# Last feed-forward stage of a transformer block: its buffers, routing and first two samples' work placed among the last slots of attention

## The reference

```python
x = x + 0.5 * ffn(layernorm(x), Wr, br, W1, b1, W2, b2)
x = x + attention(layernorm(x), Wqkv, Wo)          # 16 heads of 16, rotary, causal
x = x + 0.5 * ffn(layernorm(x), Wr, br, W1, b1, W2, b2)

def ffn(x, ...):                  # per sample b:
    scores0 = x[:, 0, :] @ Wr + br                 # routing by row 0 of a sample
    _, idx = top_k(scores0, 2)                     # 2 of 8 experts
    h = gelu(x @ W1[idx] + b1[idx])                # 256 -> 2 x 256
    return sum_k(h @ W2[idx] + b2[idx]) / 2
```

## Time and profile before

| | |
|---|---|
| median of 3 runs | 2322.23 us (2321.12 to 2323.56) |
| the profiled execution, its own time | 2318.06 us |
| its span, first to last instruction | 2316.4 us |
| PE busy | 2134.5 us, 92% |
| DVE, ACT, POOL busy | 1919.7, 1358.9, 1299.7 us |
| mean granted clock of TensorE | 0.987 |
| attention's last slots and the join | about 1845 to 1961 us of the span |

### The profile page before, as it was taken

How to read it: one execution, slowest core, us unless ns; L and a number is a source line. 1 busy time by engine, 2 the same in 40 slices (tenths; PEclk the granted TensorE clock), 3 DMA queues, 4 the chain that set the end, 5 groups by cost and what they waited for, 6 DMA issues and landing times. The chain is left out here.

```text
span 2316.4 us, 53401 instructions
## 1 busy us (share of the span) xinstructions
PE 2134.5 (92%) x18194; PEld 1160.0 (50%) x18194; DVE 1919.7 (83%) x3973; ACT 1358.9 (59%) x2568; POOL 1299.7 (56%) x1460
## 2 busy tenths in 40 slices
PE   5999998799999999999999999999999986999999
PEld 2666665344444444444444444444444434666666
DVE  6777776688999899899989998998999854777776
ACT  4545544166667666666666666666667653555553
POOL 6666666454555455455545545554555435666664
PEclk9999999899999999999999999999999988999999
DMA  6766665444445434444544454444445413666665
GB/s 206 205 199 204 199 194 183 109 88 88 96 98 100 95 93 97 88 92 93 102 90 95 96 99 92 92 97 88 93 98 100 89 56 119 194 203 200 203 204 165
DMA packets 280391, 295.32 MB, mean 127 GB/s; under 512 B 45784, under 2 KB 263224, under 8 KB 280120
## 3 DMA queue, kind: packets, MB, share of 16 engines
q1 hardware_dynamic: 280120, 291.90, 50.1%
HBM read 140.08 MB, written 83.89 MB: 97 GB/s over the span
## 5 line engine op out<-in xcount | busy, mean ns | idle before, releaser
L996 ACT ACTIVATE probs<-bank 128x512 f32<-128x512 f32 x1280 | 747.8, 603 | 460.5 <-PE bank L1104 454.1
L929 DVE TENSOR_REDUCE at_mx<-bank 128x1 f32<-128x512 f32 (+3 forms) x1408 | 838.8, 634 | 137.9 <-PE bank L1086 137.9
L850 POOL TENSOR_SCALAR_AFFINE_SELECT probs<-probs 128x512 f32<-128x512 f32 x512 | 320.4, 638 | 671.4 <-ACT probs L996 667.7
L1104 PE MATMUL bank<-stacks 49*128 49x512 f16 (+3 forms) x2048 | 460.9, 303 | 72.9 <-ACT probs L996 70.9
L1081 PE MATMUL bank<-stacks 48*128 48x512 f16 (+3 forms) x2048 | 491.2, 302 | 26.0 <-DVE at_mx L929 13.1
L587 ACT ACTIVATE probs<-bank,b1s 128x512 f32<-128x512 f32 x256 | 176.1, 688 | 371.2 <-PE bank L652 362.7
L1104 PEld LDWEIGHTS bank<-stacks 49*128 49x128 f16 x2048 | 136.1, 94 | 461.0 <-ACT probs L996 338.3
L1086 PE MATMUL bank<-mask,turn 64*128 64x128 bf16 (+2 forms) x1408 | 341.0, 242 | 0.0
L652 PE MATMUL bank<-stacks 128*128 128x512 f16 x768 | 175.5, 386 | 25.4 <-DVE stacks L529 25.3
L1081 PEld LDWEIGHTS bank<-stacks 48*128 48x128 f16 x2048 | 157.7, 94 | 72.3 <-DVE at_mx L929 47.0
L856 POOL TENSOR_TENSOR turned<-turned,at_sin 128x512 f32<-128x512 f32 x128 | 176.5, 1379 | 30.8 <-DVE turned L904 30.8
(11 more groups left out here) (127 smaller groups left out, 4071.5 us busy)
## 6 DMA issues: line engine op xcount, KB each, us to landing
stacks<-qk_image SPq DMA_DIRECT2D x384, 128.0 KB, 4.5
qk_image<-v_qk SPq DMA_DIRECT2D x128, 256.0 KB, 4.1
stacks<-w_hi SPq DMA_DIRECT2D x192, 128.0 KB, 3.7
stacks<-w_lo SPq DMA_DIRECT2D x192, 128.0 KB, 3.8
b2s<-in_b SPq DMA_DIRECT2D x128, 128.0 KB, 3.9
after_ffn<-probs SPq DMA_DIRECT2D x32, 512.0 KB, 6.5
at_x<-after_ffn SPq DMA_DIRECT2D x32, 512.0 KB, 4.0
late_x<-after_ffn SPq DMA_DIRECT2D x32, 512.0 KB, 4.7
```

The source lines that it names most:

```text
L850: nc.gpsimd.affine_select(out=ap, in_=ap, compare_op=ALU.is_ge, fill=0.0, base=0, pattern=[[0, d] for d in dims] + [[1, P]], channel_multi ...
L929: nc.vector.tensor_reduce(o_ap, i_ap, AX_X, ALU.max).then_inc(max_done, 1)
L996: nc.scalar.activation(probs[:, c, :], st_ps[c % 2][:], ACT.Exp, scale=DH ** -0.5).then_inc(exp_done, 1)
L1104: ins = nc.tensor.matmul(bank[:, col:col + T - q0], k_stack[ss.par][rows, j + ha, kt * P:(kt + 1) * P], q_stack[ss.par][rows, j + ha, q0:T ...
```

## The change

Buffers: `of_last_ffn` lays the last stage's W1, W2 and xT buffers on `stacks0`, `h` on the half of `v0_qk` that held q and k, `h32` and two of `res` on `turned`, the third of `res` on `probs`; sample 31 uses none of the stacks among these, so most waits name sample 30 now. The ones row gets a tile of its own. Routing on PE and DVE is cut into three pieces, and the first two samples' work moves to earlier slots:

| after slot | PE | DVE | ACT | POOL | SP |
|---|---|---|---|---|---|
| 120 | | | | | inputs, x(0), x(1) |
| 123 | | route_rows, norm_stats(0) | | route(0) | |
| 124 | route_turn | route_turned | | norm(0) | |
| 125 | route_logits | route_top, norm_stats(1) | | | |
| 126 | transposes(0) | xT_low(0) | xT_high(0) | norm(1) | routes, load_first(0) |
| 127 | | | | | load_second(0) |
| 128 | times_w1(0), j 0 to 2 | | | | load_first(1) |
| 129 | times_w1(0), j 3; transposes(1) | xT_low(1) | xT_high(1) | residual(0) | load_second(1) |
| 130 | times_w1(1) | norm_stats(2), h_low(0) | gelu(0) | norm(2) | load_x(2) |
| 132 | transposes(2), times_w2(0), route(1) | step(1) ... | step(1) ... | step(1) ... | load_x(3), finish, rows(1), step(1) ... |

The core of the diff (what is left out changes names only):

```diff
+    def of_last_ffn(self):
+        s0, s1 = self.stacks[0][:, 0:8, :], self.stacks[0][:, 8:16, :]
+        bits = self.v0_qk[:].bitcast(F16).rearrange("p (j n) -> p j n", n=T)
...
+        xT = [self.xT0, Split(s0[:, 4:6, :], s0[:, 6:8, :])]
+        w1 = [self.w1_0, Split(s0[:, 0:2, :], s0[:, 2:4, :])]
+        w2 = [Split(s1[:, 4 * i:4 * i + 2, :], s1[:, 4 * i + 2:4 * i + 4, :]) for i in range(2)]
+        h32 = [self.turned[:, j, :] for j in range(4)]
+        h = [Split(bits[:, 8 * i:8 * i + 4, :], bits[:, 8 * i + 4:8 * i + 8, :]) for i in range(2)]
...
             if before and s == 1:
-                sp.wait_ge(before.st_done, 40 * B)
+                sp.wait_ge(before.st_done, 40 * (B - 1))
...
             if before and s == 0:
-                act.wait_ge(before.pv_done, 16 * B)
+                act.wait_ge(before.pv_done, 16 * (B - 1))
+                act.wait_ge(before.qk_lo, 4 * B)
...
             if before and s == 1:
+                pe.wait_ge(before.res_done, 2 * (B - 1))
+            if before and s == 2:
                 pe.wait_ge(before.res_done, 2 * B)
...
-            for j in range(4):
+            for j in js:
+                if before and s == 0 and j == 0:
+                    pe.wait_ge(before.max_done, 44 * B)
+                    pe.wait_ge(before.mt_copied, 4 * B)
+                if before and s == 0 and j == 3:
+                    pe.wait_ge(before.exp_done, 40 * B)
...
-            if n.b == B - 1:
-                pe.wait_ge(own.next.xT_lo, NC)
+            if n.b >= B - 2:
+                pe.wait_ge(own.next.xT_lo, NC * (n.b - B + 3))
...
@@ vector
-            at.slot(At(0, B), 0)
-            f2.route(0)
+            for g in range(1, 4):
+                at.slot(At(0, B - 2), g)
+            f2.route_rows(0)
             f2.norm_stats(0)
+            at.slot(end, 0)
+            f2.route_turned(0)
+            at.slot(end, 1)
+            f2.route_top(0)
             f2.norm_stats(1)
-            at.slot(At(0, B), 1)
+            at.slot(end, 2)
             f2.xT_low(0)
...
+            at.slot(over, 1)
+            f2.xT_low(1)
+            at.slot(over, 2)
+            f2.norm_stats(2)
+            f2.h_low(0)
+            at.slot(over, 3)
+            at.slot(over + 1, 0)
+            for s in range(1, B):
                 f2.step(s)
@@ tensor
+            f2.route_turn(0)
+            at.slot(end, 1)
+            f2.route_logits(0)
+            at.slot(end, 2)
             f2.transposes(0)
+            at.slot(end, 3)
+            at.slot(over, 0)
+            f2.times_w1(0, range(3))
+            at.slot(over, 1)
+            f2.times_w1(0, range(3, 4))
+            f2.transposes(1)
+            at.slot(over, 2)
+            f2.times_w1(1)
+            at.slot(over, 3)
+            at.slot(over + 1, 0)
+            f2.transposes(2)
+            f2.times_w2(0)
+            f2.route(1)
+            for s in range(2, B):
                 f2.step(s)
```

More of the change, by code:

```diff
@@ L442, in sync @@
         at = Turns()
[L443 removed]
+        at.rows, at.inputs, at.routes, at.load_x, at.step, at.store, at.finish = rows, inputs, routes_of, load_x, step, store, finish
+        at.first, at.second, at.first_ahead, at.second_ahead = first, second, first_ahead, second_ahead
         return at
@@ L518, in route @@
             nc.vector.max_index(top_i[0:n, :], top[0:n, :], logits[0:n, :]).then_inc(r_top, 1)
+        def route(k):
+            route_rows(k)
+            route_turned(k)
+            route_top(k)
         def norm_stats(s):
@@ L560, in vector @@
         at = Turns()
-        at.route, at.norm_stats, at.xT_low, at.step, at.output = route, norm_stats, xT_low, step, output
+        at.route, at.norm_stats, at.xT_low, at.h_low, at.step, at.output = route, norm_stats, xT_low, h_low, step, output
+        at.route_rows, at.route_turned, at.route_top = route_rows, route_turned, route_top
         return at
@@ L671, in times_w2, with step @@
                     ins.then_inc(y_done, 1)
-        def rest(s):
+        def step(s):
+            times_w1(s)
             if s + 1 < B:
@@ L1281, in main @@
         def main(at):
-            for c in range(B):
+            for c in range(B - 2):
                 for g in range(4):
                     at.slot(At(0, c), g)
+            at.slot(At(0, B - 2), 0)
+        end, over = At(0, B - 1), At(0, B)
         @block.sync
@@ L1396, in _ @@
             main(at)
-            at.slot(At(0, B), 0)
-            at.slot(At(0, B), 1)
-            f2.xT_high(0)
-            at.slot(At(0, B), 2)
-            at.slot(At(0, B), 3)
-            at.slot(At(0, B + 1), 0)
-            for s in range(B):
+            for g in range(1, 4):
+                at.slot(At(0, B - 2), g)
+            at.slot(end, 0)
+            at.slot(end, 1)
+            at.slot(end, 2)
+            f2.xT_high(0)
+            at.slot(end, 3)
+            at.slot(over, 0)
+            at.slot(over, 1)
+            f2.xT_high(1)
+            at.slot(over, 2)
+            f2.gelu(0)
+            at.slot(over, 3)
+            at.slot(over + 1, 0)
+            for s in range(1, B):
                 f2.step(s)
```

122 lines of the change are left out of this document (72 added, 50 removed).

## The result

The changed kernel takes 2332.68 us (median of 16 runs, 2324.38 to 2341.15) against 2325.93 of the kernel before in the same session (16 runs, 2319.73 to 2329.93): ratio 1.0026, 95% interval 1.0016 to 1.0037. A second session gave 1.0031 (1.0019 to 1.0042). So it is 6 to 7 us slower, 0.3%, with both intervals above 1; the forecast was 0.9 us faster. In the kernel after, L975 are the maxima, L1127 their scores, L698 W1, L716 W2, L679 the last stage's transposes, L106 statistics, L355 the load of x.

The account below looks back on a forecast made before the run. PE was taken to be held up around the join, by waits for routing and sample 2's load and statistics, and by half clock. 12.7 + 0.4 - 7.3 - 0.2 - 4.7 = 0.9 us off 2322.23: 2321.3, range 2315.5 to 2327.

Parts of the forecast that it names:

- I take them as shifted as a whole: Last stage's later steps: they keep their order and distances, so nothing is gained or lost there.
- DVE's work between maxima: Slots 124 to 127: work between maxima n = 10 and n = 0 stops PE; slot 128 starts 7.3 us later.
- The clock: Slots 124, 126 and times_w1(1): PE's waits lower the granted clock, costing 1.4 us twice and 1.9, sum 4.7.
- A: Whole changed part: the clock stays up, 5.6 us gained, 2316.6 us; chance 0.20.
- Rival B: Slots 124 and 126: low-clock stretches last, each costing 3.9 us in place of 1.4; 2326.3 to 2330 us; chance 0.14.
- From the store to W1 of step 2: Behind sample 31's store: the chain to times_w1(2) takes 16.5 us instead of 29.2, a gain of 12.7.
- From slot 128 to the store: Slot 128 to sample 31's store: 38.8 us without the clock term, 0.4 less than before.
- Rival D: Last stage: statistics wait for x in later steps too, so the join's gain is lost, 2322.2 us; chance 0.08.
- Rival C: Slots 124 to 127 absorb half the 7.3 us on DVE and the long waits go; 2315 down to 2313; chance 0.10.

Follow-up runs that it names:

- e3: Kernel after with 9 and 12 idle matmuls on PE ahead of the maxima's scores n = 2 in slots 124 and 126; ratio to the kernel before 0.9987.
- r1_after: The kernel after, unchanged, run and profiled once more; ratio to the kernel before 1.0031.
- e4: Kernel after with statistics of sample 3 behind xT_low(2), W1 of step 2 loaded ahead of sample 31's store, second routing behind step 4; ratio to before 0.9988.
- e6: Kernel after with the edits of e4 and e5 together; ratio to the kernel before 0.9929.
- e2: Kernel before with idle statistics, some 2.9 us, added on DVE ahead of slots 124 and 126; ratio to the kernel before 1.0041.
- e8: Kernel after with x(s + 3) loaded ahead of load_first(s + 1) in every step of the last stage; ratio to the kernel before 0.9956.
- r2_after: The kernel after, unchanged, profiled once more; one run, W1 of step 31 457.37 us behind the mark in slot 124.
- e5: Kernel after with DVE's routing and statistics cut up inside slots 123 to 127, ahead of maxima that wait for PE; ratio to the kernel before 0.9971.
- e1: Kernel before with only the last stage's new buffer places, the ones row's own tile and the waits they need; ratio to the kernel before 0.9997.
- e7: Kernel before with statistics of sample 2 behind h_low(0) and xT_low(1), and W1 of step 1 loaded ahead of slot 130; ratio to it 0.9983.
- e10: Kernel before with x(s + 3) loaded ahead of load_first(s + 1) in every step of the last stage; ratio to the kernel before 0.9937.

## Why the prediction was wrong

The sum on record was: slots 7.3 and clock 2.8 later, from slot 128 to W1 of step 2 11.0 earlier (12.7 + 0.4 - 0.2, less 1.9 of clock), nothing behind it: 0.9 gained. Measured, as means of the three profiles of the kernel after against before: 13.1 later; 9.7 earlier (9.9, 8.1 and 11.1, from 67.90 before to 57.98, 59.85, 56.81); 3.2 later (3.7, 2.0, 3.8). Together 6.6 later, which is what the medians say. Of the 7.5 us between forecast and measurement, 3.4 are the clock in the slots, 3.2 the later steps of the stage, and 1.3 the way from slot 128 to `times_w1(2)`; the delay on DVE gives 0.4 back. So two steps of the prediction failed, the size of the clock term and "I take them as shifted as a whole".

- **DVE's work between maxima: right.** 7.3 forecast (its four terms add up to 7.4), 6.9 by e3. PE waits 2.08 and 2.60 us in the two slots named.
- **The clock: right in kind, wrong in size; the first step that failed.** That it falls in slots 124 and 126 was right, and A's time with the clock up is refuted. The size in the slots was "3.3 and 3.4 us", 1.4 twice, so 2.8; measured are 3.3, 8.0 and 7.4 in the three profiles, 6.2 in the mean. It was taken from short stretches of the trace, while slot 129 of the earlier trace rows, low all through, was made a bound. Five profiles have low stretches of 3.4 to 20.5 us there, and four lose over 7 us. Rival B's mechanism, at 0.14, is what usually happens in the slots (7.8 by its price of 3.9 for each slot; 7.3 to 8.0 measured). Its total, 4.1 to 7.8 us slower, holds the 6 to 7 measured, which is in part luck, since it had no loss in the stage. In the join the fall was forecast inside `times_w1(1)`, 7.20 us for the group. It came there in two of the three profiles (7.03 and 6.98); in the first the group runs at full clock (5.34) and the low stretch stands at the end of slot 129 and in `transposes(1)` (1.70 for eight), and r1_after has both.
- **From the store to W1 of step 2: right.** 16.35 us (1943.00 to 1959.35), and 16.59 and 16.37 in the other two, against 16.5. Store to load took 2.99, load to statistics 3.26, the wait was 9.20. The wait of 11.16 was moved and not removed. It is a matter of order: e4 takes it away by moving the statistics of sample 3, the second routing and one load of W1.
- **From slot 128 to the store: 42.2 against 40.7** (38.8 and 1.9 of clock). The table load to the second pair of GELUs took 2.45 (2.46 forecast), PE's wait 2.01 (1.95). The forecast was 1.5 us more than before; counted from the turn of the maxima in slot 128 it is 2.9, 4.6 and 1.7 more in the three profiles, with 6.8, 10.2 and 3.4 us at the low clock on the way. e6 has the same order there and no low stretch, and takes 38.8 against 38.7 before. So what is over is the low clock.
- **"I take them as shifted as a whole": wrong, the second step that failed.** The later steps were put at nothing and lost 2.0 to 3.8 us. Rival D had the mechanism (statistics waiting for x), not the size. e2 shows that a kernel with the stage's old code loses them too, e8 that the loads carry them: x(6) landed 7.2 instead of 6.0 us behind its issue, PE waited 2.27 us (1.10 before) for what hangs on it, the clock fell behind that wait, and step 5 took 12.99. Why that one load is slower stays open. It took 7.2 to 7.3 us in five profiles (after, r1_after, r2_after, e2, e5) and 5.8 to 6.0 in before, e1 and e7, with the same loads ahead of it and at the same distance from W1 of step 4. How late the kernel comes to it doesn't decide: e5 issues it at 1975.2, ahead of before (1976.4), and has it slow, e1 at 1979.5 and has it fast. In e3 it took 5.8, but was issued 1.2 us later against W1 of step 4, and step 5 took 12.99 too.
- **Rival C** (slots absorb the work) is refuted for this place, and true for others in the same slots: e5.

The rule of thumb of the Trainium skill ("TensorE: Matmul & The Clock Gate", section "HAM oscillation — how this bites in real kernels"), by which pauses as short as these leave the clock up, does not hold here: the granted clock fell to 0.50 at 1854.6, at the end of a wait of 2.08 us, and at 1875.1, inside one of 2.60.

## What to carry to other kernels

Work put on an engine that another waits for costs its length only where that engine has no gap: look for the maxima (or whatever it serves) ahead of which it already waits, and put the pieces there; 10 to 15 us became 1.2, 4.3 and 6.0 so, in three profiles. A wait of 2 us inside dense TensorE work is to be priced with a low clock that lasted 3 to 20 us here, and with the worse of these unless a trace of that place shows otherwise. When a wait is a matter of one engine's order, change the order first: the change laid the buffers anew and moved work of all five engines, while one move on SP in every step of the stage gave 15 us (e10) and one on DVE, with a load of W1 ahead of it, 4 (e7). Do not size such a term, or take the rest of a kernel as unmoved, from one profile.

## What the runs showed of the hardware

The granted clock is not a function of the kernel alone. e5 and e6 have the same program up to slot 128, on PE no wait above 0.5 us in slots 124 and 125; in e5 the clock stayed at 1.00 there, in e6 it was 0.50 for 10.2 us from 1857.3 on and slot 128 came 4.9 us later. The kernel after's slots scatter in the same way, and its runs spread wider: 2324.38 to 2341.15, against 2319.73 to 2329.93 before. Its fastest run has the highest mean granted clock (0.985), its slowest the lowest (0.975). That the slots make this spread is likely, not shown.

That PE has work again did not end a low stretch here: in the longest one, of r1_after, PE was busy 19.05 of 20.50 us, and the clock stayed at 0.50 throughout.

A load of x (128x1024 f32) for sample 6 took 5.8 to 7.3 us from its issue to the first statistic where it stands behind the loads of W1 and the biases (eleven profiles), and 3.3 behind the store of sample 31, where nothing else was in flight when it was issued. Issued ahead of the loads of W1 (e8), the loads of x landed after 3.3 to 5.2 us.
